# Macaron block on one core: both halves of the gate logits in one stage, the second kept raw, and new orders of three parts of the program

## The chip, the core and the metric

The kernel runs on one core of a Trainium2 chip. The metric is the device time of one execution in microseconds (us), lower is better. The core has a matrix engine (PE, with its weight loads shown apart as PEld), a vector engine (DVE), a scalar engine (ACT), a third elementwise engine (POOL) and SP, which here only issues DMA transfers. The engines run side by side and wait for one another through semaphores. PE writes its results to PSUM, which DVE and ACT can read; everything else works on SBUF.

## What is computed

For x of 8 batches x 512 tokens x 128 channels:

```
x = x + 0.5 * ffn(layernorm(x))
x = x + attn(layernorm(x))
x = x + 0.5 * ffn(layernorm(x))

attn:  q, k = rmsnorm(x Wq), rmsnorm(x Wk);  v = x Wv          (16 heads of 64)
       gate_logits = einsum('bthd,hd->bht', k, u / |u|) / sqrt(64)
       bias = -dist * omega_eff[head] * softplus(gate_logits)   (causal)
       y = softmax(q k^T / sqrt(64) + bias) v;  out = y Wproj
ffn:   two matrices W1, W2, each changed by products of 16 tokens of the batch; gelu between
```

## The kernel before

**The batch is the loop.** Each of the 8 batches goes through stages. The names of stages below are those of the tables in the code: `zt` turns the normalized tokens, `m`, `h`, `out` are the feed-forward network (`"a"` the one ahead of attention, `"c"` the one behind it), `qk q t` projects four heads' queries and keys for 128 tokens, `v j t` the values, `gl hf` the gate logits of half `hf` of the heads (8 of them), `gr hf` turns the finished gates into rows, `t p` turns the normalized queries and keys of a pair, `a h` makes the scores of head h for their row maxima, `nm` turns the maxima, `s h` makes head h's scores again, `pv h` multiplies their exponentials with the values, `wp i` is the output projection of four heads, `yx` turns the last pair's output.

**The order is written by hand.** `ORDER` has a list of stages for each engine and for each of the parts lead, first (batch 0), body (batches 1 to 6), final (batch 7). An engine does its list strictly in order; a stage of an engine waits for what it needs from the others. The lists interleave two batches (and the end of a third): `THIS`, `NEXT` and `LAST` say whose stage it is. So PE works on head 9's scores of one batch among the projections of the next.

**The ring.** All stages but `s` and `pv` get their PSUM from a ring of four banks, in the order of PE's list. `UNITS` says how many each takes (`a` 3, `t` 2, `h` 4, `gl` 1). PE may fill a bank only when DVE or ACT has taken what stood in it four units before.

**Precision by three products.** `product` computes a matrix product as high x high + high x low + low x high, three matmuls into one bank. A `gl` stage does so for each of four blocks of 128 tokens, with 8 columns of `wu`, so 12 matmuls of 8 columns.

**The gate's way.** DVE's `take_logits` waits for PE and for the inverse root mean squares of the keys of the half (ACT's `qkn`), multiplies the logits of the bank by them into `lg` and gives the bank back. ACT's `gate_softplus` (four small instructions, `lga`, `lge`, `lgp`, `lgl`) follows, then POOL's `gates` (four), PE's `gr` and DVE's copy to `gtt` (`take_gate_rows`), and two DMA issues of SP for each of two quarters of the heads (`gd`), which PE's `a` of these heads waits for. The half 0 is made with the projections of the first heads, the half 1 at the end of the batch's part, on PE after `a 6`.

**Low parts.** POOL makes `pt_l`, the low part of the exponentials of each head (`pl h`), which `pv h` needs, besides `w_l` (`m`), `hid_l` (`h`) and `ytt` (`yt`). In the last batch DVE makes one of three parts of `pt_l`, and all three of head 15.

Of the kernel before, what the change touches and what calls it, by code (L numbers as in the profile page):

```python
# [70 lines left out]
            ("qk", 1, 2, NEXT), ("m", "c", LAST), ("pv", 9, THIS), ("qk", 1, 3, NEXT), ("v", 0, 0, NEXT),  # L71
            ("v", 0, 1, NEXT), ("gl", 0, NEXT), ("v", 0, 2, NEXT), ("s", 11, THIS), ("t", 0, NEXT), ("t", 1, NEXT),
            ("pv", 10, THIS), ("wp", 1, THIS), ("t", 2, NEXT), ("v", 0, 3, NEXT), ("s", 12, THIS), ("gr", 0, NEXT),
            ("t", 3, NEXT), ("pv", 11, THIS), ("h", "c", LAST), ("a", 0, NEXT), ("s", 13, THIS), ("a", 1, NEXT),
            ("qk", 2, 0, NEXT), ("qk", 2, 1, NEXT), ("a", 2, NEXT), ("pv", 12, THIS), ("a", 3, NEXT),
            ("qk", 2, 2, NEXT), ("qk", 2, 3, NEXT), ("s", 14, THIS), ("a", 4, NEXT), ("qk", 3, 0, NEXT),
            ("qk", 3, 1, NEXT), ("qk", 3, 2, NEXT), ("nm", 0, NEXT), ("out", "c", LAST), ("qk", 3, 3, NEXT),
            ("a", 5, NEXT), ("pv", 13, THIS), ("s", 15, THIS), ("a", 6, NEXT), ("gl", 1, NEXT), ("pv", 14, THIS),
            ("a", 7, NEXT), ("t", 4, NEXT), ("wp", 2, THIS), ("nm", 1, NEXT), ("t", 5, NEXT), ("t", 6, NEXT),
        ],  # L80
        "final": [
            ("s", 0, THIS), ("t", 7, THIS), ("gr", 1, THIS), ("pv", 15, LAST), ("v", 1, 0, THIS), ("s", 1, THIS),
            ("v", 1, 1, THIS), ("pv", 0, THIS), ("a", 8, THIS), ("s", 2, THIS), ("pv", 1, THIS), ("a", 9, THIS),
            ("s", 3, THIS), ("pv", 2, THIS), ("a", 10, THIS), ("s", 4, THIS), ("pv", 3, THIS), ("wp", 3, LAST),
            ("a", 11, THIS), ("s", 5, THIS), ("pv", 4, THIS), ("nm", 2, THIS), ("v", 1, 2, THIS), ("v", 1, 3, THIS),
            ("s", 6, THIS), ("a", 12, THIS), ("pv", 5, THIS), ("s", 7, THIS), ("pv", 6, THIS), ("a", 13, THIS),
            ("s", 8, THIS), ("pv", 7, THIS), ("s", 9, THIS), ("a", 14, THIS), ("wp", 0, THIS), ("a", 15, THIS),
            ("pv", 8, THIS), ("zt", "c", LAST), ("s", 10, THIS), ("pv", 9, THIS), ("nm", 3, THIS), ("s", 11, THIS),
            ("pv", 10, THIS), ("m", "c", LAST), ("wp", 1, THIS), ("s", 12, THIS), ("pv", 11, THIS), ("s", 13, THIS),
            ("pv", 12, THIS), ("s", 14, THIS), ("pv", 13, THIS), ("s", 15, THIS), ("h", "c", LAST), ("pv", 14, THIS),  # L90
# [25 lines left out]
            ("qk", 0, 3, NEXT), ("qkn", 0, 1, NEXT), ("yt", 3, THIS), ("qk", 1, 0, NEXT), ("s", 9, THIS),
            ("qk", 1, 1, NEXT), ("v", 0, 0, NEXT), ("v", 0, 1, NEXT), ("qk", 1, 2, NEXT), ("qk", 1, 3, NEXT),
            ("qkn", 1, 0, NEXT), ("qkn", 1, 1, NEXT), ("v", 0, 2, NEXT), ("nm", 3, THIS), ("gate", 0, NEXT),
            ("t", 0, NEXT), ("t", 1, NEXT), ("s", 10, THIS), ("v", 0, 3, NEXT), ("s", 11, THIS), ("t", 2, NEXT),
            ("t", 3, NEXT), ("s", 12, THIS), ("qk", 2, 0, NEXT), ("yt", 4, THIS), ("s", 13, THIS), ("qk", 2, 1, NEXT),  # L120
            ("qk", 2, 2, NEXT), ("yt", 5, THIS), ("qkn", 2, 0, NEXT), ("qk", 2, 3, NEXT), ("qk", 3, 0, NEXT),
            ("s", 14, THIS), ("qk", 3, 1, NEXT), ("nm", 0, NEXT), ("qkn", 2, 1, NEXT), ("qk", 3, 2, NEXT),
            ("qkn", 3, 0, NEXT), ("qk", 3, 3, NEXT), ("s", 15, THIS), ("qkn", 3, 1, NEXT), ("yt", 6, THIS),
            ("gate", 1, NEXT), ("t", 4, NEXT), ("nm", 1, NEXT), ("t", 5, NEXT), ("t", 6, NEXT),
        ],
        "body": [
            ("t", 7, THIS), ("yt", 7, LAST), ("s", 0, THIS), ("v", 1, 0, THIS), ("v", 1, 1, THIS), ("s", 1, THIS),
            ("ln1", "a", NEXT), ("v", 1, 2, THIS), ("ln2", "a", NEXT), ("s", 2, THIS), ("zt", "a", NEXT),
            ("s", 3, THIS), ("yt", 0, THIS), ("m", "a", NEXT), ("s", 4, THIS), ("v", 1, 3, THIS), ("yt", 1, THIS),
            ("s", 5, THIS), ("h", "a", NEXT), ("ln1", "c", LAST), ("ln2", "c", LAST), ("s", 6, THIS), ("nm", 2, THIS),  # L130
            ("zt", "c", LAST), ("ln1", "att", NEXT), ("s", 7, THIS), ("ln2", "att", NEXT), ("yt", 2, THIS),
# [3 lines left out]
            ("qk", 1, 3, NEXT), ("v", 0, 0, NEXT), ("v", 0, 1, NEXT), ("qkn", 1, 0, NEXT), ("qkn", 1, 1, NEXT),  # L135
            ("v", 0, 2, NEXT), ("gate", 0, NEXT), ("t", 0, NEXT), ("t", 1, NEXT), ("s", 11, THIS), ("m", "c", LAST),
            ("t", 2, NEXT), ("v", 0, 3, NEXT), ("s", 12, THIS), ("t", 3, NEXT), ("h", "c", LAST), ("yt", 4, THIS),
            ("qk", 2, 0, NEXT), ("qk", 2, 1, NEXT), ("yt", 5, THIS), ("s", 13, THIS), ("qk", 2, 2, NEXT),
            ("qk", 2, 3, NEXT), ("qkn", 2, 0, NEXT), ("qk", 3, 0, NEXT), ("s", 14, THIS), ("qk", 3, 1, NEXT),
            ("qk", 3, 2, NEXT), ("qkn", 2, 1, NEXT), ("nm", 0, NEXT), ("qk", 3, 3, NEXT), ("qkn", 3, 0, NEXT),  # L140
            ("qkn", 3, 1, NEXT), ("s", 15, THIS), ("gate", 1, NEXT), ("t", 4, NEXT), ("yt", 6, THIS), ("nm", 1, NEXT),
            ("t", 5, NEXT), ("t", 6, NEXT),
# [156 lines left out]
def macaron(nc: bass.Bass, x, Wq, Wk, Wv, Wproj, q_rms_w, k_rms_w, omega, u, W1, b1, W2, b2, scale, out):  # L299
# [23 lines left out]
    with ExitStack() as ctx:  # L323
# [1322 lines left out]
```

## Time and profile before

| | |
|---|---|
| runs | 761.49 us median of 3 (760.38 to 761.83) |
| profiled execution | 761.77 us, of which 759.9 us from the first to the last instruction |
| instructions | 25094, of them 9299 matmuls |
| busy | PE 731.5 us (96%), DVE 656.4 (86%), POOL 645.7 (85%), ACT 640.2 (84%) |
| granted clock of PE | 0.996 of full speed over the span |

The profile shows one execution. An engine is busy while one of its instructions runs; a matmul's shown length is longer than the distance to the next one, since they overlap, so the distance of two starts tells what a matmul costs PE. A wait is printed behind the instruction that waited, with the instruction that released it. Times in the rows count from the first instruction.

### The profile page before, as it was taken

Reading aid. Unit: us, or ns where it says so; the run is one execution under the profiler, and the core shown is the slowest. Engines: PE = TensorE matmul, PEld = TensorE weight load, DVE = VectorE, ACT = ScalarE, POOL = GpSimd, SP = SyncE. Lnnn points to the kernel's source line nnn. Section 1 sums busy time; section 2 is a strip of 40 time slices with the busy share of each in tenths; the row PEclk is TensorE's granted clock in tenths of the full one; section 3 lists DMA queues with packets and bytes.
Section 4 is the critical chain, followed back from the end, with each engine's and each line's share of the span. In section 5 each row is a group of like instructions: output and inputs, shape, how many; then the busy total and the mean of one; then the engine's idle time right before and its main releaser. Section 6 shows DMA issues by size and latency. Waiting matters only on the chain.

```text
span 759.9 us, 25094 instructions
## 1 busy us (share of the span) xinstructions
PE 731.5 (96%) x9299; PEld 526.1 (69%) x9299; DVE 656.4 (86%) x2105; ACT 640.2 (84%) x1420; POOL 645.7 (85%) x753
## 2 busy tenths in 40 slices
PE   4889999999999999999999999999999999999987
PEld 2356767677767777687667777577776876777765
DVE  8799888988988888988989889897889879899976
ACT  5768888888998889887998889988898879986673
POOL 6537879989998989989899899989899899997690
PEclk9989999999999999999999999999999999999999
DMA  5332424253343514454143532435133430534431
GB/s 153 61 87 70 87 44 103 56 100 73 62 96 85 101 30 91 89 101 92 26 105 71 100 73 54 103 80 108 29 86 89 108 88 21 109 72 105 95 44 30
DMA packets 99618, 60.33 MB, mean 79 GB/s; under 512 B 74622, under 2 KB 86400, under 8 KB 99496
## 3 DMA queue, kind: packets, MB, share of 16 engines
q1 hardware_dynamic: 99336, 58.19, 36.1%
q8 instruction: 75, 1.23, 0.7%
q10 hardware_dynamic: 160, 0.52, 0.3%
q14 instruction: 47, 0.39, 0.2%
HBM read 4.74 MB, written 2.10 MB: 9 GB/s over the span
## 4 chain that ended last, share of the span: by engine, by line
PE 67%; DVE 14%; ACT 13%; issue 4%; POOL 2%; DMA 1%; DVEq 0%; ACTq 0%; POOLq 0%
PE ps L1089 12%; PE ps L1090 11%; PE ps L1091 11%; PE ps L1220 7%; PE ps L1246 7%; PE ps L1247 7%; PE ps L1202 5%; DVE masked L1588 4%; ACT qk L1025 3%; PE ps L1248 3%; DVE ss L1553 3%; ACT pt L1050 2%; PE ps L1106 1%; ACT hid L967 1%; ACT qkn L978 1%
## 5 line engine op out<-in xcount | busy, mean ns | idle before, releaser
L845 POOL TENSOR_TENSOR pt_l<-pt 128x512 f16<-128x512 f32 x366 | 321.4, 906 | 34.4 <-ACT pt L1050 32.5
L1588 DVE CUSTOM_DVE_ANT_0 masked<-ps,causal_row 128x512 f16<-128x512 f32 x448 | 192.1, 486 | 26.0 <-PE ps L1220 25.1
L1050 ACT ACTIVATE pt<-ps 128x512 f32<-128x512 f32 (+1 forms) x384 | 174.8, 535 | 17.2 <-PE ps L1248 15.1
L871 POOL TENSOR_TENSOR qkn<-qkn,rs 128x512 f32<-128x512 f32 x128 | 129.9, 1043 | 28.9 <-ACT rs L989 28.3
L1246 PE MATMUL ps<-qk 128*128 128x512 f16 (+3 forms) x512 | 146.6, 299 | 0.0
L1247 PE MATMUL ps<-qk 128*128 128x512 f16 (+3 forms) x512 | 146.5, 299 | 0.0
L1089 PE MATMUL ps<-v_buf,pt 128*128 128x65 f16 x1280 | 129.8, 194 | 2.6 <-POOL pt_l L845 1.2
L1090 PE MATMUL ps<-v_buf,pt 128*128 128x65 f16 x1280 | 129.8, 193 | 0.0
L1091 PE MATMUL ps<-v_buf,pt_l 128*128 128x65 f16 x1280 | 129.6, 193 | 0.0
L1089 PEld LDWEIGHTS ps<-v_buf,pt 128*128 128x128 bf16 x1280 | 118.0, 98 | 8.4 <-issue 4.9
L1090 PEld LDWEIGHTS ps<-v_buf,pt 128*128 128x128 bf16 x1280 | 117.5, 98 | 1.8
L1091 PEld LDWEIGHTS ps<-v_buf,pt_l 128*128 128x128 f16 x1280 | 117.5, 97 | 0.0
L1248 PE MATMUL ps<-causal_t,ident 128*128 128x128 f16 x512 | 105.5, 219 | 0.0
L1220 PE MATMUL ps<-qk 96*128 96x512 f16 (+3 forms) x512 | 97.1, 299 | 1.6 <-ACT qkn L978 0.5
L849 POOL TENSOR_TENSOR ytt<-ytok,ytt 128x512 f16<-128x512 f32 x63 | 74.0, 1176 | 19.8 <-ACT ytt L1065 18.4
L977 ACT ACTIVATE sq<-ps 128x512 f32<-128x512 f32 x128 | 77.5, 606 | 14.1 <-PE ps L1091 13.4
L1553 DVE TENSOR_REDUCE ss<-sq 128x8 f32<-128x512 f32 x128 | 82.8, 679 | 4.4 <-ACT sq L977 4.2
L978 ACT ACTIVATE qkn<-ps 128x512 f32<-128x512 f32 x128 | 78.1, 610 | 0.0
L1089 PE MATMUL ps<-wqkv_h,zt_h_att 128*128 128x512 f16 x192 | 73.0, 380 | 1.7 <-ACT qkn L978 0.8
L1091 PE MATMUL ps<-wqkv_h,zt_l_att 128*128 128x512 f16 x192 | 72.7, 379 | 0.0
L1090 PE MATMUL ps<-wqkv_l,zt_h_att 128*128 128x512 f16 x192 | 72.7, 379 | 0.0
L1220 PEld LDWEIGHTS ps<-qk 96*128 96x128 f16 x512 | 44.1, 97 | 40.2 <-issue 4.8
(212 smaller groups left out, 1966.6 us busy)
## 6 DMA issues: line engine op xcount, KB each, us to landing
qk<-qk SPq DMA_DIRECT2D x128, 128.0 KB, 2.4
qk<-qk SPq DMA_DIRECT2D x62, 256.0 KB, 3.7
x_in<-in_L_attn_x SPq DMA_DIRECT2D x8, 256.0 KB, 3.2
out<-x_out SPq DMA_DIRECT2D x7, 256.0 KB, 2.4
qk<-qk SPq DMA_DIRECT2D x1, 1024.0 KB, 7.5
qk<-gtt SPq DMA_DIRECT2D x64, 8.0 KB
qk<-nmt SPq DMA_DIRECT2D x64, 2.0 KB
y_hl<-ytt SPq DMA_TRANSPOSE x62, 3.2
```

The lines of the kernel that those rows point to most:

```text
L845: g.tensor_tensor(pt_l[:, h % 2, c], pt[:, h % 2, c], pt_h[:, h % 2, c], ALU.subtract).then_inc(s_pt_l, 1)
L871: g.tensor_tensor(qk, qk, r.unsqueeze(4).broadcast_to([P, 2, 2, 2, D]), ALU.mult).then_inc(s_qkn, 1)
L1050: a.activation(pt[:, h % 2, c], ps[:, j, 0:width], ACT.Exp).then_inc(s_exp, 1)
L1089: pe.matmul(dst, ah, bh, start=first, stop=False)
L1090: pe.matmul(dst, ah, bl, start=False, stop=False)
L1091: return pe.matmul(dst, al, bh, start=False, stop=last)
L1220: mm = pe.matmul(dst, q1(h)[0:MROW, ib * P:keys], k1(h)[0:MROW, 0:keys], start=True, stop=by_dve)
L1246: pe.matmul(dst, k1(h)[:, keys], q1(h)[:, kb * P:T], start=True, stop=False)
L1247: pe.matmul(dst, k2(h)[:, keys], q2(h)[:, kb * P:T], start=False, stop=False)
L1248: mm = pe.matmul(dst[:, 0:P], ident16[:, :], causal_t16[:, :], start=False, stop=True)
L1553: d.tensor_reduce(ss[:, :, qd % 2, t, :], sq[:, blk % 4, :].rearrange("p (j m d) -> p j m d", j=2, d=D), AX.X, ALU.add).then_inc(s_sqsum, 1)
L1588: ins = d.tensor_tensor_reduce(masked[:, part.unit(s, i)[0], col:col + (ib + 1) * P], part.bank(s, i)[:, col:col + (ib + 1) * P], causal_r ...
```

## The change

From the second batch on, PE's stage `gl 0` multiplies with all 16 columns of `wu` at once: still 12 matmuls, each of 16 columns, written as two runs of 8 columns that lie 32 apart, so that each half stands together in the bank. The stage `gl 1` is gone from PE's lists of first and body. DVE's `gl 0` then multiplies half 0 as before, copies the raw half 1 from the bank to `lg_raw` in SBUF, gives the bank back with this copy and waits for the copy's own semaphore. DVE's `gl 1` reads `lg_raw`. ACT's `gate_softplus` waits for a semaphore of its own, `s_lg`, in place of the bank's.

```diff
         lg = sb("lg", [P, TB, HH])
+        lg_raw = sb("lg_raw", [P, TB, HH])
...
+        s_lg = sem("s_lg")
...
             def gate_softplus(part, s, b, hf):
-                part.taken(act, ("gl", *s[1:]))
+                if b == 0:
+                    part.taken(act, ("gl", *s[1:]))
+                else:
+                    act.wait_ge(s_lg, (b - 1) * 2 + hf + 1)
...
             def gate_logits(part, s, b, hf):
...
+                    if b == 0:
+                        w = slice(hf * HH, (hf + 1) * HH)
+                        mm = product(part.bank(s)[:, t * HH:(t + 1) * HH], zt_h["att"][:, c], zt_l["att"][:, c], wu_h[:, w],
+                                     wu_l[:, w])
+                    else:
+                        both = part.bank(s)[:, 0:2 * TB * HH].rearrange("p (f t n) -> p f t n", f=2, t=TB)[:, :, t, :]
+                        mm = product(both, zt_h["att"][:, c], zt_l["att"][:, c], wu_h[:, :].rearrange("p (f n) -> p f n", f=2),
+                                     wu_l[:, :].rearrange("p (f n) -> p f n", f=2))
...
             def take_logits(part, s, b, hf):
-                part.full(dve, s)
+                if b == 0 or hf == 0:
+                    part.full(dve, s)
+                    raw = part.bank(s)[:, 0:TB * HH]
+                else:
+                    raw = lg_raw[:, :, :].rearrange("p t n -> p (t n)")
                 dve.wait_ge(s_rs, (b * 2 + hf + 1) * 4)
...
+                if b == 0:
+                    part.taken_by(ins, s)
+                    return
+                ins.then_inc(s_lg, 1)
+                if hf == 0:
+                    part.taken_by(d.tensor_copy(lg_raw[:, :, :].rearrange("p t n -> p (t n)"), part.bank(s)[:, TB * HH:2 * TB * HH]), s)
+                    part.taken(dve, s)
```

All five engines' lists of first, body and final are written anew; the lead is unchanged. In the body most stages keep their place or change with a neighbour. Those that the prediction speaks of are `gl 1` and `nm 0` on PE, `gl 0` and `gr 1` on DVE, `gate 1` on ACT, and POOL's end of the last batch. Two lines of the tables, for PE's body:

```diff
-            ("a", 5, NEXT), ("pv", 13, THIS), ("s", 15, THIS), ("a", 6, NEXT), ("gl", 1, NEXT), ("pv", 14, THIS),
+            ("qk", 3, 3, NEXT), ("a", 6, NEXT), ("s", 15, THIS), ("nm", 0, NEXT), ("pv", 14, THIS), ("a", 7, NEXT),
```

**PE, end of the body's part.** L1220 is a matmul of stage `a` (one head has four), the rows with `wu` are stage `gl 1`, of which the first three of twelve stand here. Before:

```order
L1220 MATMUL ps<-qk 128x512
L1220 MATMUL ps<-qk 128x384
L1220 MATMUL ps<-qk 128x128
L1220 MATMUL ps<-qk 128x256
L1089 MATMUL ps<-wu_h,zt_h_att 128x8
L1090 MATMUL ps<-wu_l,zt_h_att 128x8
L1091 MATMUL ps<-wu_h,zt_l_att 128x8
```

After (L1257 to L1259 are the last six matmuls of `s 15`, L1239 is `nm 0`, L1095 to L1097 begin `pv 14`):

```order
L1257 MATMUL ps<-qk 128x128
L1258 MATMUL ps<-qk 128x128
L1259 MATMUL ps<-causal_t,ident 128x128
L1257 MATMUL ps<-qk 128x256
L1258 MATMUL ps<-qk 128x256
L1259 MATMUL ps<-causal_t,ident 128x128
L1239 MATMUL ps<-ident,maxima 128x128
L1095 MATMUL ps<-v_buf,pt 128x65
L1096 MATMUL ps<-v_buf,pt 128x65
```

The twelve matmuls between `a 6` and `pv 14` are gone; `s 15` stands behind `a 6` in place of ahead of it, and `nm 0`, which stood seven stages up, comes right ahead of `pv 14`.

**DVE, where the first half of the logits is taken,** in the body. The first row is a values' low part (`v`), `rden` and `ytok` are `pv 9`. Before:

```order
L1610 TENSOR_TENSOR v_buf<-ps,v_buf 128x8x64 x2
L1559 TENSOR_TENSOR lg<-ps,rs 128x32
L1610 TENSOR_TENSOR v_buf<-ps,v_buf 128x8x64
L1599 RECIPROCAL rden<-ps 128x4
L1603 TENSOR_TENSOR ytok<-ps,rden 128x4x64
```

After:

```order
L1632 TENSOR_TENSOR v_buf<-ps,v_buf 128x8x64
L1574 TENSOR_TENSOR lg<-ps,rs 128x32
L1582 COPY lg_raw<-ps 128x32
L1632 TENSOR_TENSOR v_buf<-ps,v_buf 128x8x64 x2
L1621 RECIPROCAL rden<-ps 128x4
L1625 TENSOR_TENSOR ytok<-ps,rden 128x4x64
```

The logits are taken one `v` earlier, and the copy, with its wait, is added ahead of `pv 9`.

**POOL, end of the last batch.** The `pt_l` rows are `pl 13` and `pl 14`, the `ytt` rows `yt 5` and `yt 6`, `w_l` is `m "c"`, `hid_l` is `h "c"`, both of batch 6. Before:

```order
L845 TENSOR_TENSOR pt_l<-pt 128x256
L849 TENSOR_TENSOR ytt<-ytok,ytt 128x512
L854 TENSOR_TENSOR w_l<-weff 128x512
L857 TENSOR_TENSOR w_l<-weff,w_h 128x512
L845 TENSOR_TENSOR pt_l<-pt 128x512
L845 TENSOR_TENSOR pt_l<-pt 128x256
L849 TENSOR_TENSOR ytt<-ytok,ytt 128x512
L864 TENSOR_TENSOR hid_l<-hid 128x512 x4
```

After:

```order
L848 TENSOR_TENSOR pt_l<-pt 128x256
L852 TENSOR_TENSOR ytt<-ytok,ytt 128x512
L848 TENSOR_TENSOR pt_l<-pt 128x512
L848 TENSOR_TENSOR pt_l<-pt 128x256
L857 TENSOR_TENSOR w_l<-weff 128x512
L860 TENSOR_TENSOR w_l<-weff,w_h 128x512
L852 TENSOR_TENSOR ytt<-ytok,ytt 128x512
L867 TENSOR_TENSOR hid_l<-hid 128x512 x4
```

The two `w_l` go behind `pl 14`. PE's list changes with it: `s 15`, `h "c"`, `pv 14`, `pv 15` before; `s 15`, `pv 14`, `h "c"`, `pv 15` now.

## Rows read from the trace of the kernel before

**Rows 1.** The page: span, and the chain that ended last by engine.

```profile
span 759.9 us, 25094 instructions
...
PE 67%; DVE 14%; ACT 13%; issue 4%; POOL 2%; DMA 1%; DVEq 0%; ACTq 0%; POOLq 0%
```

**Rows 2.** Busy time of each engine in one middle batch (417.49 to 506.22 us).

```profile
417.49:506.22 88.73, 88.36 (x1151) 64.06 (x1149) 77.13 (x262) 79.14 (x179) 81.00 (x92) 1.00 0.37 80
```

**Rows 3.** Waits in 477 to 507 us: engine, line, releaser; total, times, longest.

```profile
PEld ps L1089 <- DVE maxima L1588: 1.3, 4, 0.4
```

**Rows 4.** Timeline of DVE at the end of a batch, from its last idle.

```profile
496.88 0.69 DVE L1588 CUSTOM_DVE_ANT_0 masked<-ps,causal_row 128x512 f16<-128x512 f32 x1 [0.17 <-PE ps L1220]
...
501.31 0.19 DVE L1559 TENSOR_TENSOR lg<-ps,rs 128x32 f32<-128x32 f32 x1
501.41 0.68 DVE L1588 CUSTOM_DVE_ANT_0 masked<-ps,causal_row 128x512 f16<-128x512 f32 x1
```

**Rows 5.** End of the last batch: timelines of POOL, PE and DVE.

```profile
731.31 1.04 POOL L854 TENSOR_TENSOR w_l<-weff 128x512 f16<-128x512 f32 x1
732.30 1.60 POOL L857 TENSOR_TENSOR w_l<-weff,w_h 128x512 f16<-128x512 f32 x1
733.87 2.50 POOL L845 TENSOR_TENSOR pt_l<-pt 128x512 f16<-128x512 f32 x2
...
732.70 0.38 PE L1089 MATMUL ps<-zt_h_a,weff 128*128 128x512 f16 x1
...
736.63 0.19 PE L1089 MATMUL ps<-v_buf,pt 128*128 128x65 f16 x1 [1.18 <-POOL pt_l L845]
...
733.53 3.13 DVE L1502 TENSOR_TENSOR pt_l<-pt 128x512 f16<-128x512 f32 x3
```

**Rows 6.** Timeline of PE: first of the twelve gate products, and what follows.

```profile
677.09 0.17 PE L1089 MATMUL ps<-wu_h,zt_h_att 128*128 128x8 f16 x1
...
677.40 0.19 PE L1089 MATMUL ps<-v_buf,pt 128*128 128x65 f16 x1
...
678.30 0.57 PE L1220 MATMUL ps<-qk 96*128 96x512 f16 x2
```

**Rows 7.** The chain that ended last, 728 to 745 us: start, us, what.

```profile
738.52 0.19 PE ps L1089
...
741.00 0.06 PE ps L1089
```

**Rows 8.** Timeline of DVE around the first half of the logits.

```profile
469.65 0.18 DVE L1559 TENSOR_TENSOR lg<-ps,rs 128x32 f32<-128x32 f32 x1
...
470.48 0.17 DVE L1599 RECIPROCAL rden<-ps 128x4 f32<-128x4 f32 x1
470.69 0.42 DVE L1603 TENSOR_TENSOR ytok<-ps,rden 128x256 f32<-128x256 f32 x1
```

**Rows 9.** Timeline of PE, first product of head 10 after it.

```profile
471.42 0.19 PE L1089 MATMUL ps<-v_buf,pt 128*128 128x65 f16 x1
```

**Rows 10.** Timeline of ACT at the end of a batch.

```profile
501.53 0.23 ACT L1011 ACTIVATE lga<-lg 128x32 f32<-128x32 f32 x1 [0.49 <-DVE lg L1559]
```

**Rows 11.** Gate rows of one batch: timelines of DVE, SP and PE.

```profile
425.58 0.21 DVE L1570 COPY gtt<-ps 128x128 f16<-128x128 f16 x1
...
427.71 0.69 DVE L1545 SCALAR_TENSOR_TENSOR x<-ps,x_att 128x512 f32<-128x512 f32 x1
...
425.82 1.46 SPq L745 DMA_DIRECT2D qk<-gtt  x2
...
431.54 0.71 PE L1220 MATMUL ps<-qk 96*128 96x512 f16 x4
...
433.53 0.19 PE L1089 MATMUL ps<-v_buf,pt 128*128 128x65 f16 x1
```

**Rows 12.** DMA issues: KB each, median us from issue to landing.

```profile
qk<-qk SPq DMA_DIRECT2D x128, 128.0 KB, 2.4
qk<-qk SPq DMA_DIRECT2D x62, 256.0 KB, 3.7
```

More of the change, by code:

```diff
@@ L68 @@
+            ("v", 1, 3, THIS), ("pv", 3, THIS), ("s", 5, THIS), ("a", 9, THIS), ("h", "a", NEXT), ("s", 6, THIS),
+            ("a", 10, THIS), ("wp", 0, THIS), ("pv", 4, THIS), ("a", 11, THIS), ("out", "a", NEXT), ("pv", 5, THIS),
+            ("nm", 2, THIS), ("zt", "c", LAST), ("s", 7, THIS), ("pv", 6, THIS), ("a", 12, THIS), ("s", 8, THIS),
             ("zt", "att", NEXT), ("pv", 7, THIS), ("a", 13, THIS), ("qk", 0, 0, NEXT), ("s", 9, THIS),
@@ L116 @@
[L116 to L124, printed above, removed]
+            ("s", 2, THIS), ("v", 1, 1, THIS), ("t", 7, THIS), ("ln1", "a", NEXT), ("s", 3, THIS), ("yt", 0, THIS),
@@ new lines @@
+            ("v", 0, 0, NEXT), ("qk", 1, 1, NEXT), ("qk", 1, 2, NEXT), ("qk", 1, 3, NEXT), ("nm", 3, THIS),
+            ("qkn", 1, 0, NEXT), ("qkn", 1, 1, NEXT), ("v", 0, 1, NEXT), ("gate", 0, NEXT), ("t", 0, NEXT),
+            ("t", 1, NEXT), ("v", 0, 2, NEXT), ("v", 0, 3, NEXT), ("s", 10, THIS), ("t", 2, NEXT), ("t", 3, NEXT),
+            ("s", 11, THIS), ("yt", 4, THIS), ("qk", 2, 0, NEXT), ("s", 12, THIS), ("qk", 2, 1, NEXT),
+            ("s", 13, THIS), ("qkn", 2, 0, NEXT), ("qk", 2, 2, NEXT), ("qk", 2, 3, NEXT), ("qkn", 2, 1, NEXT),
@@ L125 @@
+            ("yt", 5, THIS), ("qk", 3, 0, NEXT), ("s", 14, THIS), ("nm", 0, NEXT), ("qk", 3, 1, NEXT),
+            ("s", 15, THIS), ("qk", 3, 2, NEXT), ("qkn", 3, 0, NEXT), ("qk", 3, 3, NEXT), ("yt", 6, THIS),
+            ("qkn", 3, 1, NEXT), ("t", 4, NEXT), ("nm", 1, NEXT), ("t", 5, NEXT), ("t", 6, NEXT), ("gate", 1, NEXT),
         ],
         "body": [
-            ("t", 7, THIS), ("yt", 7, LAST), ("s", 0, THIS), ("v", 1, 0, THIS), ("v", 1, 1, THIS), ("s", 1, THIS),
+            ("t", 7, THIS), ("yt", 7, LAST), ("s", 0, THIS), ("v", 1, 0, THIS), ("s", 1, THIS), ("v", 1, 1, THIS),
@@ L199 @@
[L199 to L202 removed]
+            ("pv", 15, LAST), ("t", 7, THIS), ("ln1", "a", NEXT), ("ln2", "a", NEXT), ("v", 1, 0, THIS),
@@ L259 @@
         "first": [
-            ("ln1", "a", NEXT), ("rows", 2, THIS), ("gd", 2, THIS), ("rows", 3, THIS), ("swap", 2, THIS),
-            ("yt", 0, THIS), ("yt", 1, THIS), ("back", 2, THIS), ("nm", 2, THIS), ("swap", 3, THIS), ("gd", 3, THIS),
-            ("yt", 2, THIS), ("yt", 3, THIS), ("back", 3, THIS), ("nm", 3, THIS), ("rows", 0, NEXT), ("gd", 0, NEXT),
-            ("swap", 0, NEXT), ("rows", 1, NEXT), ("gd", 1, NEXT), ("back", 0, NEXT), ("swap", 1, NEXT),
-            ("yt", 4, THIS), ("yt", 5, THIS), ("nm", 0, NEXT), ("back", 1, NEXT), ("nm", 1, NEXT), ("yt", 6, THIS),
+            ("ln1", "a", NEXT), ("rows", 2, THIS), ("gd", 2, THIS), ("swap", 2, THIS), ("yt", 0, THIS),
+            ("gd", 3, THIS), ("yt", 1, THIS), ("rows", 3, THIS), ("back", 2, THIS), ("nm", 2, THIS), ("yt", 2, THIS),
+            ("swap", 3, THIS), ("yt", 3, THIS), ("back", 3, THIS), ("rows", 0, NEXT), ("nm", 3, THIS),
+            ("gd", 0, NEXT), ("gd", 1, NEXT), ("swap", 0, NEXT), ("yt", 4, THIS), ("rows", 1, NEXT),
+            ("back", 0, NEXT), ("yt", 5, THIS), ("nm", 0, NEXT), ("swap", 1, NEXT), ("back", 1, NEXT),
+            ("yt", 6, THIS), ("nm", 1, NEXT),
         ],
@@ L1185, in gate_logits @@
                     c = slice(t * P, (t + 1) * P)
-                    mm = product(part.bank(s)[:, t * HH:(t + 1) * HH], zt_h["att"][:, c], zt_l["att"][:, c], wu_h[:, w],
-                                 wu_l[:, w])
+                    if b == 0:
[6 more added lines that the diff above has]
+                                     wu_l[:, :].rearrange("p (f n) -> p f n", f=2))
                 part.filled_by(mm, s)
```

239 lines of the change are left out of this document (117 added, 122 removed).

## The prediction

> **What bounds the kernel now.** I read the page first. The chain that ended last runs over PE for 67% of the span, over DVE for 14% and ACT for 13% [rows 1], so PE sets most of the time but hands it over now and then. The windows view says how tight that is: in a middle batch of 88.73 us PE is busy 88.36, while POOL has 81.00, ACT 79.14 and DVE 77.13 [rows 2]. A matmul taken off PE is therefore worth its full distance to the next one, except where PE has to stand and wait for another engine. The reader should look for those places next. The waits view of the last 30 us of a batch's part has the weight loads waiting four times, 1.3 us in all, for DVE's row maxima [rows 3]: PE's ring of four banks is full there, and DVE empties it. In DVE's timeline of the same place the last idle is 0.17 us ahead of head 5's maxima at 496.88; from there on its rows follow one another without idle as far as the list is shown [rows 4]. So at the end of each part DVE sets the pace, and elsewhere PE does. The last batch has stalls of its own: PE waits 1.18 us for POOL's `pt_l` at 736.63 [rows 5].
>
> **The change, part by part.** All sums are against the profiled execution (759.9 us of span, 761.77 in all); it lies 0.28 us above the median of 761.49, and I take the difference from the median. A difference of 0.2%, 1.5 us, is about what a measurement of this kernel can tell from none.
>
> *Twelve products fewer, seven times.* The twelve matmuls of `gl 1` take PE from 677.09 to 677.40 [rows 6], 0.31 us, or 0.026 each. They go in batches 1 to 7: 7 x 0.31 = 2.2 us of PE. But they stand in the stretch where DVE sets the pace. There DVE keeps its `lg` instruction, 0.10 us from start to start (501.31 to 501.41), since it still multiplies the raw half; what DVE gains comes from the new order alone. PE now has `a 5` ahead of `qk 3 3` and `s 15` behind `a 6`, so DVE's maxima are fed earlier and its last idle of 0.17 us [rows 4] can close. Bounds for this term are therefore 7 x 0 and 7 x 0.31. I take 0.27 each, nearer the upper end: PE's share of the chain is the largest, and what PE gains before the ring fills is kept in banks filled ahead, up to four; 7 x 0.27 = 1.9 us.
>
> *Sixteen columns in place of eight* in `gl 0`. The trace has 0.026 us at 8 columns [rows 6] and no row at 16. A row of 128 columns in the last chain goes by in 0.06 [rows 7]. So 84 products cost between nothing and 84 x 0.03 = 2.5 us more. I take nothing: eight columns more are a fifteenth of the way to 128. The Trainium skill's "TensorE: Matmul & The Clock Gate" (section "Back-to-back issue gap") gives about 81 ns for each matmul of 128 columns in a stream with weight loads. By it, as an estimate, the 84 products removed would be worth up to 6.8 us and the sum would come to 753.6. The trace does not agree: 0.026 us at 8 columns, 0.06 at 128.
>
> *The copy and its wait.* DVE gets seven copies of 128x32 from PSUM. The nearest row is the multiplication of the same size, 0.18 us [rows 8], of which 0.10 counts behind another instruction [rows 4]. The wait for its own semaphore costs what lies between `rden` and `ytok`: 470.48 + 0.17 to 470.69, 0.04 us, and the overlap of 0.09 with the next instruction that is lost (0.19 long, the next one 0.10 behind its start [rows 4]). Together 0.2 to 0.3 us. Queued behind it on DVE are two `v` and `pv 9`; `ytok` of `pv 9` ends at 471.11 and PE starts head 10 at 471.42 [rows 8, 9], so 0.3 us of delay is just hidden. Ahead of it the logits are taken one `v` earlier, which lets ACT start the gates sooner, and ACT holds 13% of the chain. I take nothing; the ends are 7 x 0.3 = 2.1 us lost and 7 x 0.1 gained.
>
> *ACT's gates.* `gate 1` goes behind `yt 6` and `t 4`; ACT had idled 0.49 us before it [rows 10]. ACT is not what holds PE there, and POOL takes the gates behind `yt 6` as before. Nothing.
>
> *The last batch.* POOL's two `w_l` (731.31 and 732.30) stand ahead of `pt_l` of head 14 (733.87, 2.50 us), for which PE waits until 736.63 [rows 5]. In the new order `pt_l` can start at 731.31 and ends by 733.8 with the same 2.50. PE, which has ended `s 15` at 732.70 (where `h "c"` begins now), waits till about 734.1 (the same 0.26 behind POOL's end as now), makes `pv 14` in 0.9 (677.40 to 678.30 [rows 6]), then `h "c"` in 2.6 (732.70 to 736.63 less the wait of 1.18, less 0.15 that ends overlap), whose first `w_l` is there at 734.9, and starts `pv 15` at 737.6 in place of 738.52 [rows 5, 7]: 0.9 us. The 2.50 was measured beside three low parts on DVE (733.53 [rows 5]), which come later than the new place; with less beside it `pt_l` should be some 0.4 shorter, and the gain 1.3. DVE's own part for head 15 ends at 736.66 [rows 5] and does not stand in the way, and `ytt` of `yt 6`, which the last projection needs, stays behind `w_l`, no later than now. Everything behind `pv 15` follows from it. Bounds: 0, if the rest of POOL's work comes as late as now, and 2.2, both waits of PE: 1.18 ahead of `pv 14`, and 1.0 from its end (736.63 + 0.9) to 738.52. I take 1.1.
>
> *The other moves* are changes with a neighbour, on engines that wait here and there. The whole of what PE is not busy is 88.73 - 88.36 = 0.37 us in a batch [rows 2], so they can give at most 6 x 0.37 = 2.2 us. I take nothing on the whole, since each closes one gap and may open another.
>
> The sum: 1.9 + 1.1 = 3.0, nothing for the rest; 761.49 - 3.0 = 758.5. **Forecast 758.5 us**, by itself 757.2 to 759.8.
>
> **The rivals.**
>
> *The new orders close PE's gaps too.* For it speaks that DVE's and ACT's idle slots at the places named are met by moves of just the stages that wait; against it, that a gap in an order of five engines closes at one place and opens at the next. 758.5 - 2.2 = 756.3, the 3.0 still in it. Chance 0.20.
>
> *DVE takes the gain back.* If DVE sets the pace at the end of each part wholly, the products removed are worth 0, and the copy adds its 0.2 us at each of seven places; only the last batch is left: 761.49 - 1.1 + 0 to 1.4 = 760.4 to 761.8. For it speak the waits for maxima [rows 3] and DVE's rows without idle [rows 4], against it the idle DVE has elsewhere (11 us in a batch [rows 2]). Chance 0.14.
>
> *The gate rows come late*, the case on the slower side. DVE's copy to `gtt` at 425.58 goes behind `pv 0`, one more `v` and `wp 3`, whose addition ends at 428.40 [rows 11], so 2.8 us later. SP's two pairs of transfers then start at 428.65 in place of 425.82, the second is issued by 429.4, and by the 2.4 us of the nearest transfers [rows 12] it lands at 431.8. Head 8's maxima, which need it and begin at 431.54 now [rows 11], stand one head's scores later (a head's maxima and scores together are 1.99 us [rows 11], the scores alone some 1.3), at 432.8. The margin is 1.0 us. It decides from a landing of 3.4 us on; to make the kernel slower by 0.2% seven batches would have to lose (3.0 + 1.5) / 7 = 0.64 us each, a landing of 3.4 + 0.64 = 4.0, above the 3.7 of larger transfers [rows 12]. Together with the copy's cost less is enough. 763 to 765. Chance 0.07.
>
> *Writing two separated runs is slow.* Each of the 84 products left in batches 1 to 7 writes two runs of 8 columns. If each cost as much as 128 columns, 84 x 0.03 = 2.5 us come back: 758.5 + 2.5 = 761.0. No row before has such a product. The Trainium skill's "PSUM — Partial Sum Buffer" (section "Specifications (TRN2)") says that any non-contiguous access slows matmuls significantly; no run here shows it yet. Chance 0.03.
>
> *Nothing changes:* the transfers of time between engines cancel, 761.5. Chance 0.05.
>
> **How the numbers follow.** The forecast keeps 0.51, and all of its own range is faster by over 0.2% (below 759.97). With the first rival 0.71 are faster. DVE's case, the slow writes and no change give 0.22 within 0.2%, and the gate rows 0.07 slower. The range from 756.0 to 761.0 takes in the first rival and the better part of DVE's; out of it stay the late gates, no change and a rest on the fast side, less than 2 in 10.
>
> **What the changed profile would show.** The products of 16 columns at 0.026 us from start to start, and 9215 matmuls in place of 9299; a middle batch near 88.4 us; DVE's copy near 0.18 us with 0.04 of idle behind it, and PE's head 10 not later than 0.3 us behind `ytok`; PE's wait ahead of `pv 14` about as now, 1.2 us, and `pv 15` right behind `h "c"`, about 1 us earlier against `s 15`. I am wrong if the batches stay at 88.7 (DVE's case), if PE's L1220 rows of head 8 wait for the transfers of `gtt`, or if the last batch's waits only move to another engine, `ytt` above all.

## The result and the profile after

The changed kernel takes 766.03 us (median of 6 runs, 765.11 to 767.51), the kernel before 761.84 beside it; the ratio is 1.0057, with a 95% interval of 1.0043 to 1.0072. It is slower by 4.2 us. The forecast was 758.5, its range ended at 761.0, and slower had a chance of 0.07: wrong in size and in sign.

The page of the changed kernel, against [rows 1]: the chain has moved towards PE (70% in place of 67%).

```profile
span 764.2 us, 24943 instructions
PE 735.5 (96%) x9215; PEld 525.0 (69%) x9215; DVE 661.8 (87%) x2112; ACT 643.1 (84%) x1420; POOL 644.2 (84%) x753
...
PE 70%; DVE 12%; ACT 10%; issue 3%; POOL 2%; DMA 1%; SPq 0%; DVEq 0%; ACTq 0%; POOLq 0%
```

The windows view of one middle batch of the changed kernel (length, busy time and instructions of each engine, granted clock, DMA share), which answers to [rows 2]:

```profile
419.59:509.33 89.74, 88.93 (x1139) 64.02 (x1136) 78.14 (x263) 79.68 (x180) 81.03 (x93) 1.00 0.37 79
```

The batch is 89.74 us long where it was 88.73. The clock is full in both. DVE is busy 1.01 us more (78.14 against 77.13), and its one added instruction is a copy of 0.18. That is the first thing to ask about.

A table of the parts says where the loss sits. A part is measured from the start of PE's first product in it to that of the next part's (the last one to the start of PE's last product), worked out from each trace; the middle is the mean of six batches.

| us | first part | a middle batch | last part |
|---|---|---|---|
| before | 78.88 | 88.84 | 73.03 |
| changed | 78.31 | 89.94 | 72.30 |

First and last part give 0.6 and 0.7 back. The six middle batches lose 6 x 1.10 = 6.6 us, with 0.31 us of products fewer in each. The lead, whose tables are the same, ends at 71.72 us in the trace of before and at 70.73 in that of the changed kernel; over all the traces of this case it ends between 69.4 and 71.7. I take that for scatter and not for the change; without it the two spans would differ by 5.3 us in place of 4.3.

**Where in a batch.** Most of the loss stands at one place, PE's four transposes of the second layer norm (`zt att`). The timeline of PE, of before and of changed:

```profile
452.70 0.64 PE L1106 MATMUL ps<-ident,z_att 128*128 128x128 f32 x4
```

```profile
455.36 1.39 PE L1112 MATMUL ps<-ident,z_att 128*128 128x128 f32 x4
```

From the distances of the starts PE needs 0.92 us more there than before (the expectations below say 0.96), 0.22 ahead of the first transpose and 0.70 between the four, and nearly the same in all six batches; 0.10 of it comes back right behind, at `pv 7`. The row carries no wait in brackets, since the transposes wait inside the group. The chain of the changed kernel at this place names what it waits for (start, us, what):

```profile
452.71 1.02 DVE z_hl L1447
453.73 0.07 issue
453.80 0.23 DVE od L1465
454.02 0.60 DVE zt_l_a L1468
454.62 0.08 DVE shift_att L1442
454.70 0.02 issue
454.72 0.03 ACT z_att L1006
```

The longest piece is a DVE instruction of 32 x 128 elements. DVE and POOL of the changed kernel:

```profile
452.71 1.05 DVE L1447 TENSOR_TENSOR z_hl<-z_a,z_hl 32x128 f16<-32x128 f32 x1
```

```profile
452.58 2.09 POOL L848 TENSOR_TENSOR pt_l<-pt 128x512 f16<-128x512 f32 x2 [0.79 <-ACT pt L1056]
```

and of the kernel before:

```profile
450.22 0.28 DVE L1436 TENSOR_TENSOR z_hl<-z_a,z_hl 32x128 f16<-32x128 f32 x1
```

```profile
447.44 2.61 POOL L845 TENSOR_TENSOR pt_l<-pt 128x512 f16<-128x512 f32 x3 [0.68 <-ACT pt L1050]
450.62 2.04 POOL L845 TENSOR_TENSOR pt_l<-pt 128x512 f16<-128x512 f32 x2 [0.58 <-ACT pt L1050]
```

Before, the subtraction of two operands in SBUF fell into POOL's gap from 450.05 to 450.62 and took 0.28 us. In the changed kernel it starts 0.13 us behind the start of a POOL instruction (452.58) whose end is 453.62 (two in 2.09 us), and it ends 0.14 us behind that end: 1.05 us. It is so in all six middle batches: 1.05 to 1.06 us, against 0.28 in all six of before. With the copy's 0.18 this is nearly all of DVE's 1.01 us more. The same subtraction for the first layer norm had collided in the kernel before too, so its trace held the price. Here it starts 0.56 us behind the start of a POOL instruction, and ends again 0.14 behind its end:

```profile
428.44 0.63 DVE L1436 TENSOR_TENSOR z_hl<-z_a,z_hl 32x128 f16<-32x128 f32 x1
```

By the Trainium skill's "SBUF — State Buffer" (section "Who interferes with whom") a DVE instruction with two SBUF inputs contends with a GpSimd (POOL) instruction that reads SBUF, and who comes second is blocked until the other ends. This case's traces agree where DVE comes second, 0.28 against 1.05 us, with the end 0.14 behind POOL's. One row does not fit: at 8.37 us the same subtraction takes 0.28 us in the middle of a POOL instruction on one partition (`b2rows`, 7.52 to 9.15), so not every POOL instruction blocks it.

Why it moved there: the new table gives DVE `pv 5` ahead of `ln1 att`, and `zt c` (with the subtraction in it) ahead of `ln2 att`, the small reduction `shift_att` that ACT needs to normalize. ACT's rows start at 454.72 after an idle of 1.06 us:

```profile
454.72 1.65 ACT L1006 ACTIVATE z_att<-x,shift_att,mv_att 128x128 f32<-128x128 f32 x4 [1.06 <-DVE shift_att L1442]
```

### The profile page after: what moved, and what is told of

Same layout as the page of the kernel before. It is cut to its first block, busy times and chain, and to the rows that moved or that the text cites. A ratio compares the mean times of both kernels' runs of the same rounds, so it can differ in the third digit from the quotient of the medians.

```text
span 764.2 us, 24943 instructions
## 1 busy us (share of the span) xinstructions
PE 735.5 (96%) x9215; PEld 525.0 (69%) x9215; DVE 661.8 (87%) x2112; ACT 643.1 (84%) x1420; POOL 644.2 (84%) x753
## 4 chain that ended last, share of the span: by engine, by line
PE 70%; DVE 12%; ACT 10%; issue 3%; POOL 2%; DMA 1%; SPq 0%; DVEq 0%; ACTq 0%; POOLq 0%
PE ps L1095 13%; PE ps L1096 12%; PE ps L1097 12%; PE ps L1231 7%; PE ps L1213 7%; PE ps L1257 6%; PE ps L1258 6%; ACT hid L970 3%; PE ps L1259 3%; ACT pt L1056 2%; DVE masked L1610 2%; ACT L970 2%; DVE maxima L1614 1%; POOL pt_l L848 1%; PE ps L1112 1%
## 5 line engine op out<-in xcount | busy, mean ns | idle before, releaser
L1257 PE MATMUL ps<-qk 128*128 128x512 f16 (+3 forms) x512 | 146.7, 300 | 0.0
L1095 PE MATMUL ps<-v_buf,pt 128*128 128x65 f16 x1280 | 129.8, 194 | 1.4 <-ACT pt L1056 0.6
L1097 PE MATMUL ps<-v_buf,pt_l 128*128 128x65 f16 x1280 | 129.5, 193 | 0.0
L1095 PEld LDWEIGHTS ps<-v_buf,pt 128*128 128x128 bf16 x1280 | 118.1, 98 | 6.4 <-ACT pt L1056 2.0
L1097 PEld LDWEIGHTS ps<-v_buf,pt_l 128*128 128x128 f16 x1280 | 117.6, 98 | 0.0
L1259 PE MATMUL ps<-causal_t,ident 128*128 128x128 f16 x512 | 105.6, 219 | 0.0
L1095 PE MATMUL ps<-wqkv_h,zt_h_att 128*128 128x512 f16 x192 | 73.8, 385 | 2.0 <-ACT qkn L981 1.1
L1097 PE MATMUL ps<-wqkv_h,zt_l_att 128*128 128x512 f16 x192 | 73.4, 382 | 0.0
```

The lines of the kernel that those rows point to most:

```text
L1095: pe.matmul(dst, ah, bh, start=first, stop=False)
L1097: return pe.matmul(dst, al, bh, start=False, stop=last)
L1257: pe.matmul(dst, k1(h)[:, keys], q1(h)[:, kb * P:T], start=True, stop=False)
L1259: mm = pe.matmul(dst[:, 0:P], ident16[:, :], causal_t16[:, :], start=False, stop=True)
```

## The experiments

Theories. **A**: the new orders of the middle batches cost the time, above all the late second layer norm with the long subtraction in it. **B**: the gate part costs it (copy, two runs of columns, own-semaphore wait). **C**: of the same place, ACT's order is what is late. Medians are given with the ratio to the kernel before measured on the same chip; that kernel's median was 760.73, 760.95 and 762.23 in the three groups of four. Most expectations reckon from its 761.84 of the result, so the ratio times 761.84 is what they are held against where the two differ.

### The two halves of the change

`gates_alone`: before's tables, the gate part of the change.

```diff
 (before's ORDER, "tensor", first and body)
-            ("gl", 1, NEXT)
 (gate_logits, take_logits, gate_softplus as in the change)
```

> Before's orders, with only the second gate products dropped from TensorE's list and the new gate code (16 columns, the DVE copy, ACT waiting on its own semaphore). Theory A (the new orders of the middle batches cost the time, above all those around the second layer norm; the gate part by itself gives): 759.9 to 761.8 us against 761.8. Theory B (the gate part itself costs, by the copy or by products with two separate runs of columns in PSUM): 763 or more.

Measured: 762.72 us, ratio 1.0022 (1.0008 to 1.0036). Against 761.84 that is 763.5, by which theory B holds for a part: the gate part alone costs some 0.2%, where it was to give time. Its trace, the fastest of the ten executions (761.33), doesn't show where all of it goes: against before the middle batches have 0.06 us each (88.90) and the last part 0.6.

`orders_alone`: the new tables, before's gate code.

```diff
 (the new ORDER, "tensor")
 body:   ("a", 6, NEXT),
+        ("gl", 1, NEXT),
 first:  ("pv", 14, THIS),
+        ("gl", 1, NEXT),
```

> The new orders with the old gate code, both gate products of 8 columns back on TensorE's list (behind a 6 in the middle batches, behind pv 14 in the first). Theory A: as slow as the whole change or up to 2 us slower, 766 to 768 us. Theory B (the gate part costs): 762 or less.

Measured: 771.12 us, 1.0129 (1.0114 to 1.0144). This is above theory A's range too, a miss on its upper side. The orders alone are worse than the whole change, so B can't be the main cause. The time above the whole change stands at `gl 1`, PE in one batch:

```profile
504.05 0.18 PE L1092 MATMUL ps<-wu_h,zt_h_att 128*128 128x8 f16 x1 [0.37 <-ACT qkn L981]
```

Where I put it back, the bank it needs is that of `qk 3 3`, four units ahead, which ACT gives back at 503.99 (`qkn`, 503.40, 0.59 long). From the distances of the starts PE waits 0.56 us there in each middle batch. With the 0.31 of its products this is 0.87 of the 0.95 us by which a middle batch is longer than in the changed kernel (90.89 against 89.94).

`old_middle`: the whole change, with before's body tables.

```diff
 (every engine's "body" as before; "tensor" without)
-            ("gl", 1, NEXT)
```

> The whole change, but the tables of the six middle batches are before's again (without the second gate products). Theory A: the middle batches fall back from 89.9 us each to 88.5, and the first and last part keep their 0.6 and 0.7 us: 758.5 to 760.5 us. Theory B: 765 or more. A third: the shorter first and last part of the one profile are chance, then 760.5 to 761.8.

Measured: 760.24 us, 0.9992 (0.9978 to 1.0007). Against 761.84 that is 761.2, outside theory A's range and inside the third's. But the middle batches are back at 88.87 us, and first and last part are as short as in the changed kernel (78.35 and 72.18), so they are not chance. Against `gates_alone` on the same chip only the tables of first and last part differ: 2.5 us less by the medians; in the traces, whose executions lie 1.9 apart, 0.5 of the first part, 1.4 of the last, and 1.0 of the sixth middle batch, told below.

### The second layer norm

`norm_first`: three neighbours put back in the middle batches.

```diff
 "vector" body:
-            ("pv", 5, THIS), ("ln1", "att", NEXT), ("zt", "c", LAST), ("ln2", "att", NEXT),
+            ("ln1", "att", NEXT), ("pv", 5, THIS), ("ln2", "att", NEXT), ("zt", "c", LAST),
 "scalar" body:
-            ("s", 7, THIS), ("ln1", "att", NEXT),
+            ("ln1", "att", NEXT), ("s", 7, THIS),
```

> The whole change, with three neighbours of the middle batches put back: DVE runs ln1 att ahead of pv 5 and ln2 att ahead of zt c, ACT runs ln1 att ahead of s 7. Theory A by its detail: the transposes of zt att no longer wait for ACT's normalized rows, which gives back up to six times 0.96 us of 766.0: 760.3 to 762. If instead the DMA order of SP or the other swaps set the time, it stays above 764.5.

Measured: 761.71 us, 1.0015 (1.0003 to 1.0028). Against the change's 1.0057 that is 0.42%, 3.2 us; against 761.84 it is 763.0, one above the range. The subtraction takes 0.28 us again and `zt att` waits no more; the middle batches of the trace fall from 89.94 to 89.21.

`no_second_read`: the whole change, with the two-operand instruction replaced; this leaves out the low half of 32 normalized rows.

```diff
             def first_rows_lo(part, s, b, n):
                 dve.wait_ge(s_z[n], b * TB + 1)
                 dve.wait_ge(s_z_h[n], b + 1)
+                if n == "c" and b < B - 1:
+                    d.memset(z_hl[ROWS:2 * ROWS, :], 0.0).then_inc(s_z_l[n], 1)
+                    return
```

> The whole change, but in batches 1 to 7 of the third layer norm DVE's subtraction of two SBUF operands that makes the low half of the first 32 normalized rows is left out and a memset of that half stands in its place. In the changed kernel that subtraction takes 1.05 us in each middle batch and ends 0.1 us behind the POOL instruction that it overlaps, where it took 0.28 in a gap of POOL before. Theory A with this as its main part: DVE's ln2 att comes about 0.8 to 0.9 us earlier and most of TensorE's 0.96 goes: 761 to 762.5. If the long subtraction is not on the path: above 765.

Measured: 760.77 us, 1.0002 (0.9991 to 1.0014), on the orders of the changed kernel. One DVE instruction of 1.05 us against one of 0.11, in each of six batches (the seventh had 0.28), is worth 0.55%, 4.2 us, by the ratios, and 5.5 us against `act_swap` on the same chip (below; the same orders but for one swap); the middle batches of the trace fall from 89.94 to 89.07, 5.2 us in all. DVE, PE and ACT of this run:

```profile
449.40 0.11 DVE L1449 MEMSET z_hl<- 32x64 uint32 x1
```

```profile
451.81 0.77 PE L1113 MATMUL ps<-ident,z_att 128*128 128x128 f32 x4
```

```profile
450.55 1.65 ACT L1007 ACTIVATE z_att<-x,shift_att,mv_att 128x128 f32<-128x128 f32 x4 [0.23 <-DVE shift_att L1443]
```

ACT's idle falls from 1.06 to 0.23, PE's transposes from 1.39 to 0.77. The 0.17 us by which a memset beats the undisturbed subtraction can't give this; the 0.77 of the collision can.

`act_swap`: only ACT's pair of `norm_first`.

```diff
 "scalar" body:
-            ("s", 7, THIS), ("ln1", "att", NEXT),
+            ("ln1", "att", NEXT), ("s", 7, THIS),
```

> The whole change with another single neighbour put back: ACT runs ln1 att ahead of s 7. Theory A: nothing, 765.3 to 766.5 us, since ACT's ln2 att still waits for DVE's reduction behind zt c. Theory C: 761 to 763.

Measured: 766.28 us, 1.0081 (1.0065 to 1.0097), no faster than the change. C by itself has fallen. But theory A doesn't come off whole either. DVE and ACT of this run:

```profile
453.40 0.28 DVE L1448 TENSOR_TENSOR z_hl<-z_a,z_hl 32x128 f16<-32x128 f32 x1
```

```profile
453.40 0.30 ACT L997 ACTIVATE lnv_att<-mv_att,ln_eps 128x4 f32<-128x4 f32 x1 [0.84 <-DVE mv_att L1429]
453.73 0.21 ACT L999 ACTIVATE mv_att<-lnv_att 128x4 f32<-128x4 f32 x1
453.84 1.34 ACT L1057 ACTIVATE pt<-ps 128x512 f32<-128x512 f32 x3
455.06 1.64 ACT L1007 ACTIVATE z_att<-x,shift_att,mv_att 128x128 f32<-128x128 f32 x4
```

The subtraction doesn't collide here in any middle batch, and yet they take 90.13 us on the mean (89.59 in three of them, 89.62 to 89.74 in the same three of the changed kernel). ACT now stands 0.84 us for DVE ahead of the exponentials of `s 7`. POOL's `pt_l`, made from them, is late, which is why nothing runs beside the subtraction; the normalized rows come behind them, only some 0.4 us earlier against the batch than in the changed kernel. PE stands 0.39 us less at `zt att` and 0.35 more ahead of `pv 7`. So the collision is what costs in the orders of the change, and a swap that only moves POOL away from it gives nothing.

`ln2_swap`: only one of DVE's pairs.

```diff
 "vector" body:
-            ("zt", "c", LAST), ("ln2", "att", NEXT),
+            ("ln2", "att", NEXT), ("zt", "c", LAST),
```

> The whole change with one neighbour put back: in the middle batches DVE runs ln2 att (one small reduction) ahead of zt c. Theory A (the transposes of zt att wait for ACT's ln2 att, which waits for this reduction, and that stands behind zt c on DVE): ACT's ln2 att starts 0.85 us earlier, TensorE's wait of 0.96 us per batch shrinks to about 0.1, 766.0 minus six times 0.85: 760.5 to 762. Theory C (ACT's order, s 7 ahead of ln1 att, is what is late): above 765.

Measured: 768.86 us, 1.0124 (1.01 to 1.0149), a plain miss. DVE and PE of this run:

```profile
453.62 0.16 DVE L1443 TENSOR_REDUCE shift_att<-mv_att 128x4 f32<-128x8 f32 x1 [1.01 <-ACT mv_att L999]
453.81 0.88 DVE L1448 TENSOR_TENSOR z_hl<-z_a,z_hl 32x128 f16<-32x128 f32 x1
...
454.86 0.68 DVE L1469 TENSOR_TENSOR zt_l_a<-ps,zt_h_a 128x512 f16<-128x512 f32 x1
```

```profile
455.60 0.44 PE L1113 MATMUL ps<-ident,z_att 128*128 128x128 f32 x2 [0.36 <-DVE zt_l_a L1469]
456.75 0.44 PE L1113 MATMUL ps<-ident,z_att 128*128 128x128 f32 x2 [0.72 <-DVE maxima L1611]
```

The reduction did come earlier, and ACT's rows with it (0.88 us against the batch). But DVE now waits 1.01 us for ACT ahead of it, so `zt c` behind it is later, still collides, and holds the bank of the ring that the transposes need. Two things end at this place, the normalized rows and the bank; I had seen one. The second wait of 0.72 is the ring too: `zt att` takes two banks, and four units ahead of the second stands the first of `a 12`, whose maxima DVE takes late (456.01, 0.68 long; PE goes on at 456.75).

### SP's list

DVE's `ln1 a` starts later against the batch in the changed kernel, by 0.3 to 1.1 us (1.05 in the fourth middle batch), behind the transfer of `x_in`. Theory D laid this to SP's new order.

```diff
 (every table new, "sync" body as before: swap 1, back 0 and nm 0 early again)
```

> The whole change with SP's list of DMA orders in the middle batches put back to before's. Theory D (the later back 0, swap 1 and back 1 hold up the transfer of x_in, so DVE's ln1 a starts 1.05 us later against the batch, and m a, wp 0 and add a follow it late): the waits of m a and wp 0 go, 0.4 us per batch, 763.0 to 764.3. If the order of SP costs nothing: 765.3 to 766.5.

Measured: 782.05 us, 1.0295 (1.0261 to 1.0329), a miss by 18 us. SP and PE in one batch:

```profile
507.68 0.40 SPq L784 DMA_DIRECT2D out<-x_out  x1
511.46 1.45 SPq L777 DMA_DIRECT2D qk<-nmt  x2
512.96 1.24 SPq L771 DMA_TRANSPOSE y_hl<-ytt  x1
```

```profile
516.12 0.22 PE L1096 MATMUL ps<-wp_h,y_hl 128*128 128x128 f16 x1 [2.42 <-DMA y_hl<-ytt]
```

SP idles from 508.1 to 511.5 for ACT's `nmt`, which PE's new table makes late (`nm 0` behind `s 15`); the transpose `yt 5` stands behind it, and PE's `wp 2` waits 2.6 us for it. DVE's `ln1 a` started only 0.17 us earlier in the fourth middle batch, and PE's wait at `wp 0` stayed at 0.38: the part of D that says the order of SP holds up `wp 0` has fallen. The run shows how far the tables hang together: SP's new order is needed by PE's.

### What the rest is worth

Theory E: a wait taken from PE in the third quarter of a batch shortens it. `before_t3` and `gates_t3` exchange one pair of DVE, `picked` is `old_middle` with this pair and one of PE.

```diff
 "vector" body:
-            ("pv", 11, THIS), ("t", 3, NEXT),
+            ("t", 3, NEXT), ("pv", 11, THIS),
 "tensor" body (picked alone): ("v", 1, 3, THIS) ahead of ("pv", 3, THIS)
```

> The kernel before with one pair of neighbours exchanged on DVE in the middle batches: t 3 ahead of pv 11, as in the changed kernel. Theory E (DVE waits for TensorE in the third quarter of a batch and TensorE for DVE at its end; what comes to DVE earlier ahead of a 0 shortens the batch): TensorE's wait of 0.28 us before h c goes and the batch is 0.2 to 0.3 us shorter, 759.2 to 760 against 760.95. If DVE's end is set elsewhere: no change.

> The gate part alone (as in gates_alone, 762.7 us) with the same exchange of t 3 and pv 11 on DVE. Theory E: 1.2 to 1.8 us less than gates_alone, 760.9 to 761.5. If the twelve products taken away were still worth time once DVE is earlier: less than that, down to 759.5.

> The gate part, the new first and last part, and the old tables of the middle batches with two moves of the new ones kept: DVE runs t 3 ahead of pv 11, TensorE runs v 1 3 ahead of pv 3. Each takes away a wait of TensorE that the changed kernel doesn't have (0.28 and 0.13 us per batch): 760.2 of old_middle less up to 2.4, 757.8 to 759.5 us, faster than both kernels. If DVE's end of the batch holds it: 760.2.

Measured: 761.29 us, 0.9988 (0.9976 to 0.9999); 762.11, 1.0007 (0.999 to 1.0023); 760.61, 0.9983 (0.9971 to 0.9994). In the traces PE's 0.28 us at `h c` goes in all three, and its wait at the next stage, `a 0`, grows from 0.25 (before) or 0.29 (`gates_alone`) to 0.57: the middle batches are no shorter (88.91, 88.96, 89.03). By the traces E has fallen; the wait moved one stage on. The ratios leave a little room: each of the three is 0.09 to 0.15% under the kernel it was made from (1, 1.0022 and 0.9992), and for `before_t3` that is the edge of what E forecast, but a difference of this size is within the intervals or at their end. `picked` is faster than the kernel before by 0.17%; `old_middle`, with the same first and last part, had 0.08%, and the two intervals overlap.

`copy_five`: what does the added copy cost?

```diff
                 if hf == 0:
+                    for i in range(4):
+                        d.tensor_copy(lg_more[:, i, :], part.bank(s)[:, TB * HH:2 * TB * HH]).then_inc(s_more, 1)
+                    dve.wait_ge(s_more, b * 4)
                     part.taken_by(d.tensor_copy(lg_raw ...
```

> As gates_alone, but DVE copies the raw logits five times instead of once (four times into a tile that nobody reads), to size the cost of DVE's added copy. If the copy is hidden, as predicted, by DVE's waits behind it: the median of gates_alone, 762.2 to 763.2, and middle batches of 88.7 us. If it passes into the time: four times about 0.12 us in seven batches, 3.4 us more, 766.

Measured: 763.36 us, 1.0018 (1.0003 to 1.0032), beside 1.0022 for `gates_alone`: no difference. Five of the six middle batches are 0.05 to 0.40 us longer, four of them by 0.2 or more; PE waits 0.31 more at `t 1` and 0.14 at `pv 10`, and 0.23 less at `a 0`. By the trace four copies pass some 0.2 us per batch on, so one passes about 0.05, an estimate. The last part of this one trace is 1.2 us longer, for which I have no reason.

## Why the prediction was wrong

**"Twelve products fewer", 1.9 us: mis-sized, 0.** The products went (9215 matmuls). In `gates_alone` a middle batch takes 88.70 to 88.72 us in four of six cases, as the 88.73 of [rows 2], and by the medians that kernel is 0.22% slower, not faster. Against before PE waits 0.24 us more ahead of `pv 14`, which needs DVE's `ytok` of head 13, 0.22 more at `t 4` and 0.15 less at `a 7`: together 0.31, the whole time of the twelve products. The prediction had read that DVE sets the pace there [rows 3, 4] and still took 0.27 of 0.31, from banks filled ahead. The rival "DVE takes the gain back" had this mechanism. The zero holds for the old orders: in the new ones the same stage, put back in `orders_alone`, costs 0.95 us a batch, since it brings its wait with it.

**Sixteen columns, nothing: right**, and with it the rival on separated runs. PE of the changed kernel, first and last of the twelve and what follows:

```profile
469.39 0.17 PE L1095 MATMUL ps<-wu_h,zt_h_att 128*128 128x16 f16 x1
469.42 0.17 PE L1096 MATMUL ps<-wu_l,zt_h_att 128*128 128x16 f16 x1
...
469.67 0.17 PE L1097 MATMUL ps<-wu_h,zt_l_att 128*128 128x16 f16 x1
469.69 0.38 PE L1095 MATMUL ps<-wqkv_h,zt_h_att 128*128 128x512 f16 x1
```

0.30 us for twelve, as at 8 columns [rows 6].

**The copy, nothing: right in size.** DVE of the changed kernel:

```profile
472.74 0.19 DVE L1574 TENSOR_TENSOR lg<-ps,rs 128x32 f32<-128x32 f32 x1 [0.23 <-ACT rs L992]
472.84 0.18 DVE L1582 COPY lg_raw<-ps 128x32 f32<-128x32 f32 x1
473.06 1.29 DVE L1632 TENSOR_TENSOR v_buf<-ps,v_buf 128x512 f16<-128x512 f32 x2
```

0.18 us with 0.04 idle behind. What the prediction took for a gain, the logits one `v` earlier, shows a wait of 0.23 for ACT's row scales. PE stands 0.25 us at `t 0` and 0.1 more at `pv 10` behind it; that this pair of neighbours is the cause was argued and not tried.

One thing in the gate part was not in the prediction: `lg` of the second half now reads two operands in SBUF, and so can collide with POOL itself. In `gates_alone` it did in the sixth middle batch, DVE and POOL:

```profile
677.15 0.82 DVE L1577 TENSOR_TENSOR lg<-lg_raw,rs 128x32 f32<-128x32 f32 x1
```

```profile
675.88 2.04 POOL L877 TENSOR_TENSOR qkn<-qkn,rs 128x512 f32<-128x512 f32 x2
677.88 1.04 POOL L851 TENSOR_TENSOR pt_l<-pt 128x512 f16<-128x512 f32 x1
```

0.82 us in place of 0.19, and the end 0.05 behind POOL's. This batch took 89.70 us in place of 88.71, with PE's wait at `t 4` at 1.07 in place of 0.44. Part of it (0.35, at `pv 14`) was late already. `gates_t3` has the same in its sixth middle batch (0.82 us, 89.78); no other trace has it in that batch.

**The last batch, 1.1: right.** `pv 15` starts 5.91 us behind the start of `s 15` where it was 7.13, straight behind `h c`, and POOL's two rows of `pt_l` ahead of it take 2.06 in place of 2.50, as foretold. But `s 15` comes 0.5 us later into the last part than before, so the part gives 0.7.

**"The other moves": the step that failed.** It took nothing for them, with a bound on the gain, "at most 6 x 0.37", and none on the loss. They cost the middle batches about 6.2 us, 6 x (89.94 - 88.90, the mean of `gates_alone`). The collision of DVE and POOL at one spot makes 5.2 of it by the traces of the changed kernel and `no_second_read` (4.2 by their ratios). The trace of before had the subtraction at 0.28 in POOL's gap and at 0.63 beside POOL. I priced moves by their length where they stood and didn't ask what runs beside them in the new place, though the prediction itself reckoned that POOL's `pt_l` gets shorter with less of DVE beside it in the last batch.

The bound was wrong too. Rows of PE overlap, so a wait shorter than the overlap doesn't show as idle time. From the distances of the starts, each held against the shortest usual distance behind a product of its shape, I estimate that PE stands 2.3 us in a middle batch of before and 3.6 in one of the changed kernel, where the windows view leaves 0.37 and 0.81 not busy.

**The gate rows** (the one rival on the slower side) did not come late: PE has no wait at `a 8`. The sign was right, the mechanism another.

**What stays open.** With the layer norm mended (`norm_first`) a middle batch takes 89.21 us, 0.37 over before. PE's waits at `wp 0` (0.28 more) and `t 0` (0.25 more) stand ahead of it; the likely moves, `zt a` behind `pv 1` and `gl 0` ahead of `v 0 1` on DVE, have no measurement. Nor is it shown where the 0.22% of `gates_alone` goes.

## What to carry to other kernels

When a written order is changed, list the DVE instructions with two SBUF operands and see for each which POOL instruction will run beside it in the new place; here its price was what was left of that POOL instruction. A product taken off PE in a stretch where another engine sets the pace can be worth nothing, even if PE is busy 99%; and a wait of PE that is taken away moves to the next stage until the engine that feeds it has work earlier. Bound the loss of a re-ordering as well as its gain, and take neither bound from PE's busy share: look at the distances of its starts.

## What the runs showed that I had not expected

- A DVE subtraction of 32 x 128 elements with both operands in SBUF takes 0.28 us alone and 1.05 us when it starts 0.13 us behind the start of a POOL instruction of 1.04 us; it ends 0.14 behind POOL's end. The 128 x 32 multiplication takes 0.19 and 0.82.
- The price depends on when the subtraction starts within POOL's instruction of 1.04 us: begun 0.13, 0.31 and 0.56 us behind its start (the changed kernel, `ln2_swap`, before) it takes 1.05, 0.88 and 0.63, with its end 0.14 behind POOL's each time. Begun in POOL's gap, 0.40 us ahead of the next start (450.22 and 450.62), it pays nothing.
- A row `x4` of PE can hold a wait of 0.7 us that no view puts in brackets; only its length against that of before (1.39 against 0.64) shows it.
